# A graph layer on one core: each node's edge to itself leaves the gathered lists and is computed on the chip

## The reference

```
ht = einsum('nd,rdo->nro', h, W_rel[l])
h_rel = segment_sum(ht[src, etype], dst) + h @ W_loop[l] + b_rel[l]
z = (h @ W_gat[l]).reshape(n, H, DH)
el = sum(z * attn_l[l]);  er = sum(z * attn_r[l])
e = leaky_relu(el[src] + er[dst], 0.2)
alpha = softmax of e over the edges of one dst
h_gat = segment_sum(alpha * z[src], dst) + b_gat[l]
hc = concat([h_rel, h_gat]) @ W_fuse + b_fuse      (layer 0: hc *= sigmoid(gate))
h = relu(hc)
```

## Time and profile before

| | |
|---|---|
| runs | 3487.19 us median of 3 (3486.21 to 3488.84) |
| profiled execution, span of its instructions | 3490.2 us |
| POOL | 2489.3 us busy (71%), of them 2475 gathers with 0.95 us each |
| DVE | 2380.3 us busy (68%) |
| PE, ACT | 689.4 us (20%), 424.8 us (12%) |
| first gather of layers 0 and 1 | 214.45 us, 1315.70 us |
| mean over the 16 DMA engines | 145 GB/s |

### The profile page before, as it was taken

The page is one execution under the profiler, slowest core; times in us unless marked ns, Lnnn a source line. Parts: engine busy times, 40 slices in busy tenths (PEclk is TensorE's granted clock), DMA queues, the critical chain, the costliest instruction groups (busy, mean ns, idle before and its releaser), DMA issues.

```text
span 3490.2 us, 18122 instructions
## 1 busy us (share of the span) xinstructions
PE 689.4 (20%) x1897; PEld 372.5 (11%) x1897; DVE 2380.3 (68%) x3226; ACT 424.8 (12%) x769; POOL 2489.3 (71%) x2642
## 2 busy tenths in 40 slices
PE   8942111222122230011121111221000000000000
PEld 5421000111011110000000000110000000000000
DVE  8536666677676764665777756674776788877786
ACT  3530110111111120101111111111000000000000
POOL 1457777777777756777777777775777777777776
PEclk9965555555655555555555555555555555555555
DMA  7774444455545544444454544454433333333332
GB/s 271 315 249 129 134 147 152 152 151 152 152 152 159 168 145 118 130 151 152 151 152 151 153 152 152 152 173 140 107 106 107 107 106 107 106 106 107 106 103 74
DMA packets 143244, 505.96 MB, mean 145 GB/s; under 512 B 44277, under 2 KB 51002, under 8 KB 133618
## 3 DMA queue, kind: packets, MB, share of 16 engines
q0 software_dynamic: 130032, 444.45, 43.4%
q1 hardware_dynamic: 13186, 61.24, 4.5%
HBM read 341.05 MB, written 164.51 MB: 145 GB/s over the span
## 4 chain that ended last, share of the span: by engine, by line
POOL 45%; issue 29%; DVE 10%; DMA 6%; PE 4%; POOLq 3%; DVEq 1%; ACT 1%; SPq 1%; ACTq 0%
POOL meta_nat L594 20%; POOL late L594 14%; POOL scratch L594 10%; DVE acc L1381 3%; PE ps_table L886 1%; DMA late<-table,stage_mid 1%; DMA table<-rows 1%; DMA scratch<-table,stage_tail 1%; DVE late L1377 1%; DVE scratch L1377 1%; DVE meta_nat L1377 1%; POOLq L369 1%; POOL table L671 1%; DMA meta_nat<-table,stage_head 1%; PE ps_cnt L919 1%
## 5 line engine op out<-in xcount | busy, mean ns | idle before, releaser
L594 POOL DMA_INDIRECT meta_nat<-table,stage_head x1200 | 1139.0, 949 | 395.7 <-issue 385.3
L594 POOL DMA_INDIRECT late<-table,stage_mid x720 | 681.9, 947 | 219.4 <-issue 217.9
L594 POOL DMA_INDIRECT scratch<-table,stage_tail x555 | 525.9, 948 | 175.5 <-issue 175.2
L1025 PE MATMUL ps_mix<-ident,hr 128*128 128x128 f32 x75 | 35.5, 473 | 1991.2 <-DVE hg L1401 1991.2
L788 ACT ACTIVATE ps_cnt<-logit 128x68 f32<-128x68 f32 x189 | 43.7, 231 | 2767.1 <-DVE logit L1363 2766.1
L1381 DVE TENSOR_REDUCE acc<-meta_nat 128x132 f32<-128x2112 f32 x75 | 290.6, 3875 | 8.1 <-DVE meta_nat L1377 0.5
L1371 DVE TENSOR_REDUCE acc<-meta_nat 128x128 f32<-128x2048 f32 x75 | 282.6, 3767 | 0.0
L1049 PE MATMUL ps_table<-wrel,hT 128*128 128x512 f32 x400 | 266.4, 828 | 0.0
L1353 DVE TENSOR_TENSOR raw<-late,er_cur 128x64 f32<-128x64 f32 x45 | 12.0, 267 | 324.5 <-DMA late<-table,stage_mid 324.5
L1025 PEld LDWEIGHTS ps_mix<-ident,hr 128*128 128x128 f32 x75 | 13.6, 182 | 2039.8 <-DVE hg L1401 2039.8
L1381 DVE TENSOR_REDUCE acc<-scratch 128x132 f32<-128x1188 f32 (+1 forms) x69 | 208.7, 3024 | 7.1
(11 more groups left out here) (237 smaller groups left out, 1701.4 us busy)
## 6 DMA issues: line engine op xcount, KB each, us to landing
table<-rows SPq DMA_DIRECT2D x25, 2080.0 KB, 7.7
meta_nat<-table,stage_head POOLq DMA_INDIRECT x1200, 2.8
late<-table,stage_mid POOLq DMA_INDIRECT x720
scratch<-table,stage_tail POOLq DMA_INDIRECT x555, 2.8
meta<-meta_ranked SPq DMA_DIRECT2D x1, 2438.0 KB, 15.1
wrel<-in_L_gnn_W_rel POOLq DMA_DIRECT2D x2, 1024.0 KB, 13.5
meta_nat<-in_x SPq DMA_DIRECT2D x1, 832.0 KB, 18.4
table<-rows,stage_id POOLq DMA_INDIRECT x50, 7.8
```

The source lines that it names most:

```text
L594: pool.indirect_dma_start(out=slots[b][:, k, :], out_offset=None, in_=table[l % 2], in_offset=bass.IndirectOffsetOnAxis(ap=index, axis=0)) ...
L1025: pe.transpose(mix[0], hr[:], ident[:])
```

## The change

The last slot of a node's list is compared with the node's own rows of the table. If it is one of them, and the node's rank is 128 or more, the slot is taken out of the list and of the count, and its relation (0 to 15) is kept in a new column M_SELF of `meta`, otherwise -1. For tiles 1 to 24 of every layer:

- z and `el` of each node's own row are kept on the chip (`self_z`, in the room of `rows[1]`) and copied to slot 0 of the head buffer at the tile's start. The head group now works on 17 slots. Where a node has no dropped edge, its logit there is lowered by 1e34, which makes its weight zero.
- The own message is the row of the 16 products that M_SELF names. ScalarE copies each of the 16 products of 128x128 from PSUM with a factor of 1 or 0 for each node (`own_messages`), and TensorE sums the 16 results with identity matmuls, behind the loop product, in one bank (`own`). ScalarE copies the sum to M_LOOP of `meta` (`own_sum`), where the loop product stood.
- For layers 1 and 2 this follows `next_rows` in layers 0 and 1. For layer 0 the pass over the ranked tiles is gone; in its place `first_layer_own` makes x transposed, the products with the 16 relations, `er`, own z and own message of one tile. It runs for tiles 0 and 1 ahead of the first tile and for tile t+1 behind tile t of layer 0.
- The output `yo` lies in the room of the relation weights.

```
@@ list of the edges, on VectorE, for each of three chunks @@
+                step(v.tensor_tensor(codes, lists, is_last[:, t0:t1], ALU.mult))
+                step(v.tensor_reduce(code, codes, AX.X, ALU.add))
+                step(v.tensor_tensor(gap, code, self_at[:, t0:t1], ALU.subtract))
...
+                v.tensor_tensor(codes, is_last[:, t0:t1], bc_last(dropped[:, t0:t1], ELL), ALU.mult)
...
+                v.scalar_tensor_tensor(lists, lists, float(NULL), codes, ALU.add, ALU.subtract).then_inc(s_ell_ok, 1)
@@ ScalarE @@
-            transposed_x(1)
-            for t in range(T):
-                if t < T - 1:
-                    transposed_x(t % 2)
-                act.wait_ge(s_er_ps, t + 1)
-                s.activation(meta[:, t, M_ER:META], ps_er[t % 2], ACT.Copy).then_inc(s_er, 1)
+            def own_messages():
+                for r in range(R):
+                    m = s.activation(self_rows[:, r], ps_table[:, r * D:(r + 1) * D], ACT.Copy,
+                                     scale=type_cur[:, r:r + 1])
+                m.then_inc(s_masked, 1)
+            def own_sum(t, ready):
+                act.wait_ge(s_own_ps, n_own)
...
+                s.activation(meta[:, bass.ds(t, 1), M_LOOP:META], self_sum.rearrange("p (o f) -> p o f", o=1), ACT.Copy
+                             ).then_inc(ready, 1)
+            def first_layer_own(t):
+                s.activation(x_cur[:].rearrange("p (o f) -> p o f", o=1), meta[:, bass.ds(t, 1), M_X:M_ELL], ACT.Copy
+                             ).then_inc(s_x_cur, 1)
+                act.wait_ge(s_rank_xT, n_first)
+                s.activation(hT[1][:], xT_ranked, ACT.Copy).then_inc(s_hT[1], 1)
+                act.wait_ge(s_first_ps, n_first)
+                act.reg_add(n_first, n_first, 1)
+                own_er_and_z(t).then_inc(s_er, 1)
+                own_messages()
+                own_sum(t, s_own0)
...
+                    with act.Fori(1, T - 1) as t:
+                        tile(l, t)
+                        first_layer_own(t + 1)
@@ TensorE @@
+            def own(l, k):
+                pe.wait_ge(s_masked, n_own)
...
+                pe.matmul(self_sum, hT[k][:], wz[:, l, ER:ZW], start=True, stop=False)
+                for r in range(R):
+                    mm = pe.matmul(self_sum, ident[:], self_rows[:, r], start=False, stop=r == R - 1)
+                mm.then_inc(s_own_ps, 1)
+            def first_layer_own():
...
+                pe.transpose(xT_ranked, x_cur[:], ident[:]).then_inc(s_rank_xT, 1)
+                pe.wait_ge(s_hT[1], n_hT[1])
...
+                pe.matmul(ps_z[:, 0:ER], hT[1][:], wz[:, 0, 0:ER], start=True, stop=True)
+                for c in range(4):
+                    mm = pe.matmul(ps_table[:, 512 * c:512 * c + 512], hT[1][:],
+                                   wrel[:, 0, c * RC * D:(c + 1) * RC * D], start=True, stop=True)
+                mm.then_inc(s_first_ps, 1)
+                own(0, 1)
...
-                    z_product(l + 1, 0, ZW)
+                    z_product(l + 1, 0, ER)
...
+                    own(l + 1, 0)
@@ VectorE, start and end of a tile @@
+                v.tensor_copy(slots["H"][:, 0:1, D:ROW], self_z[:, bass.ds(t, 1), :])
...
+                if l == 0:
+                    dve.wait_ge(s_own0, n_t)
```

More of the change, by code:

```diff
@@ L21 @@
 LEAST = -1.0e37
+SHUT = -1.0e34
 SLOPE = 0.2
@@ L46, in gnn_kernel @@
     META = M_LOOP + D
-    ZW = D + H + H + D
+    EL = D + H
+    ER = EL + H
+    ZW = ER + D
     HB = 25
@@ L121, in gnn_kernel @@
         rows = [sb(f"rows{i}", [P, R, ROW]) for i in range(2)]
+        self_z = rows[1][:].rearrange("p r f -> p (r f)")[:, 0:T * EL].rearrange("p (t f) -> p t f", f=EL)
+        assert T * EL <= R * ROW
+        self_rows = sb("self_rows", [P, R, D])
+        self_room = self_rows[:].rearrange("p r d -> p (r d)")
+        is_last = self_room[:, 0:T * ELL // 2].bitcast(BF16).rearrange("p (t j) -> p t j", t=T)
+        last_at, self_at, apart, may_drop, last_code, is_self, dropped = (
+            self_room[:, T * ELL // 2 + i * T:T * ELL // 2 + (i + 1) * T] for i in range(7))
+        assert T * ELL // 2 + 7 * T <= R * D
+        self_type = sb("self_type", [P, T, R])
+        no_self = sb("no_self", [P, T])
+        type_cur = sb("type_cur", [P, R])
+        shut_cur = sb("shut_cur", [P, 1])
+        x_cur = attn_tmp
         degree = sb("degree", [P, T])
@@ L816, in next_rows @@
                     s.activation(rows[0][:, :, D:ROW], bc(ps_z[:, 0:D + H], R), ACT.Copy)
-                    for j in range(2):
-                        evacuate_half(0, j)
-                    s.activation(meta[:, bass.ds(t, 1), M_ER:META],
-                                 ps_z[:, D + H:ZW].rearrange("p (o f) -> p o f", o=1), ACT.Copy).then_inc(s_rows, 1)
+                    evacuate_half(0, 0)
+                    evacuate_half(0, 1).then_inc(s_rows, 1)
                     act.reg_add(n_tab, n_tab, 1)
+                    own_er_and_z(t)
+                    own_messages()
             n_stored = counter(act, "act_stored", 16)
@@ L855, in _ @@
                 act.wait_ge(s_saved[k], 16 * (T // 2 + 2 - k))
+            act.wait_ge(s_meta_first, 16)
+            act.wait_ge(s_own_type, 1)
+            first_layer_own(0)
+            first_layer_own(1)
+            act.wait_ge(s_meta, 16)
+            act.wait_ge(s_own_type, 2)
             n_last = counter(act, "act_last_tile", 0)
@@ L859, in _ @@
                 tile(l, 0, first=True)
-                with act.Fori(1, T) as t:
-                    tile(l, t)
+                if l == 0:
+                    with act.Fori(1, T - 1) as t:
+                        tile(l, t)
+                        first_layer_own(t + 1)
+                    tile(l, T - 1)
+                else:
+                    with act.Fori(1, T) as t:
+                        tile(l, t)
                 transposed(l)
@@ L998, in _ @@
                 natural_tile(t, t % 2, next_x=t < T - 1)
[L1001 to L1017 removed]
+            def first_layer_own():
+                pe.wait_ge(s_x_cur, n_x_cur)
+                pe.reg_add(n_x_cur, n_x_cur, 1)
+                pe.transpose(xT_ranked, x_cur[:], ident[:]).then_inc(s_rank_xT, 1)
+                pe.wait_ge(s_hT[1], n_hT[1])
+                pe.reg_add(n_hT[1], n_hT[1], 1)
+                pe.matmul(ps_z[:, 0:ER], hT[1][:], wz[:, 0, 0:ER], start=True, stop=True)
[4 more added lines that the diff above has]
+                own(0, 1)
+            n_x_cur = counter(pe, "pe_x_cur", 1)
+            pe.wait_ge(s_rows, T + 1)
+            first_layer_own()
+            first_layer_own()
             pe.wait_ge(s_bload, 16 * (5 + 3 * L))
@@ L1065, in tile @@
                 next_table(l)
-            for l in range(L):
+            with pe.Fori(2, T):
+                tile(0)
+                first_layer_own()
+            tile(0)
+            tile(0)
+            for l in range(1, L):
                 with pe.Fori(0, T):
@@ L1348, in group @@
                 lo = 1 if first else 0
+                new = 1 - lo
                 dve.wait_ge(s_landed[b], n_land[b])
```

113 lines of the change are left out of this document (73 added, 40 removed).

## The result

| | before | after |
|---|---|---|
| median of the runs | 3486.7 us (3485.4 to 3488.8) | 3606.2 us (3603.2 to 3609.8) |
| ratio | | 1.0346, 95% interval 1.0331 to 1.0360: slower by 3.5% |
| profiled span | 3490.2 us | 3608.2 us, +118.0 |
| gathers | 2475 | 2403 |
| first head gather, layer 1's, layer 2's | 214.45, 1315.70, 2411.8 | 219.49, 1478.21, 2557.04 |

The account below looks back on a forecast made before the run. It took GpSimd's gathers as the bound (2475 x 1.25 = 3097 us). Layer 0 and start +203.1, layer 1 -30.0 and +10.3, layer 2 -30.0 and +0.3 gave +154: 3641 us, range 3504 to 3800.

Parts of the forecast that it names:

- The ring: Layer 0, one head exponential to the next through ScalarE and TensorE: 56.1 us for three-group tiles, 46.0 for two.
- The 15.3: Layer 0's two-group tiles, from the head's exponential to the end of the row copies, table product included: 15.3 us.
- The sum of 17: TensorE's 17 matmuls of 128x128 that sum the masked copies: 7.4 us, bounds 5.2 and 10.3.
- The masked copy: ScalarE's 128x128 copies with a factor per node: 0.25 us each, 4.1 us for 16.
- Layer 0's product: TensorE's product of tile t+1 with all relations, at the high clock: 4.3 us, bounds 4.0 and 7.6.
- the 30.7: Layer 0, own work after the row copies until the next head's exponential: 12.4 plus 18.3, together 30.7 us.
- The start: Before the gathers, 6.7 us of VectorE list work under 7.0 us of cover; second head's gathers at 262.2, not 251.61.
- Layers 1 and 2: Each layer gains 30.0 us from fewer gathers; layer 1's end adds 10.3, layer 2's last group 0.3.
- the clock's rival: TensorE's clock stays at 1.2 GHz in every burst: 3859 us, chance 0.10.
- The first rival: TensorE keeps its high clock, masked copies overlap, the chain hides behind the gathers: 3418 us, chance 0.10.
- the slots don't fall: Rival that lists get no shorter: +60 us in layers 1 and 2, 3701 us, chance 0.03.
- each us counts 48 times: Each us on a sum or on the 16 copies counts 48 times in the kernel's time, on the product 24 times.

Follow-up runs that it names:

- hidden2: Changed kernel with layer 0 reordered, the ranked tile's masked rows and sum in their own buffer and PSUM region, same results: 3433.2 us, 0.9842 of the kernel before.
- after_again: The changed kernel measured once more, nothing altered: 3607.7 us, 1.0338 of the kernel before.
- no_first_b: Changed kernel without the 16 masked copies and 16 identity matmuls of the first layer's own step: 3470.7 us, 0.9947 of the kernel before.
- no_msgs_b: Changed kernel without masked copies and identity matmuls in all layers: 3917.4 us (no_msgs 3912.3), on chips where the kernel before takes 3969.
- no_drop: Changed kernel with all own work but no list shortened: 4843.9 us, 1.2201 of the kernel before there; the same kernel on the faster chip 3675.8 us, 1.0536.

## Why the prediction was right, by its own steps

The direction, the mechanism and the place held; the size was 36 us of span too large (+154 forecast, +118.0 measured).

- **The ring** was forecast as "head exponential, 15.3, row copies, 30.7, head exponential". Measured 14.14 and 30.24, so 44.4 us for 46.0, and 54.6 for 56.1. Ten and twelve turns make 35 of the 40.6 us by which layer 1 starts earlier than forecast (+162.5, not +203.1); 2.8 came before the first turn, 2.7 at the layer's end.
- **The 15.3** was too long by the table's product. I took 6.75 us from its first instruction to the last row copy's start, from the end of layer 0. It has 5.6 (TensorE's L947 at 1217.07, the copy at 1222.70). The row chosen was the longest of its kind: the product takes 6.18 us there at a granted clock of 0.58, but 4.75 at 0.76 within the layer, and the 25 of layer 0 before lie between 4.51 and 6.18, with a mean of 5.36. In the changed kernel they lie between 4.72 and 5.13. The prediction had both rows and took the dearer one.
- **The sum of 17**: 7.4 forecast, 6.7 and 6.6 us measured from its first instruction to the copy's start at 1235.52 and 1252.73. That it came out so near is partly luck, since two terms were off in opposite ways. The burst from 1228.80 stays at a granted clock of 0.50 until 1234.0, 5.2 us and not the 4.4 assumed; its instructions are cheaper than assumed, 20 in the first 4.2 us at that clock, 0.42 us a matmul for 0.59. In hidden2, where the clock was at 1.00 throughout the sum, 34 instructions took 3.8 us, 0.11 each and so 0.22 a matmul for my 0.29; that is a quarter of the 0.45 that an instruction of 512 columns has at 1.00 in the changed kernel (L1092, eight in 3.60 us). The rule of the Trainium skill (TensorE: Matmul & The Clock Gate, Step-by-step: what each phase is for) that weight loads are pulled ahead gave an estimate of 6.3 us in the prediction (from the terms given there it is 6.1); the measurement lies between it and 7.4, and in the stream of hidden2 the trace agrees with the rule.
- **The masked copy**: 4.24 us for 16, forecast 4.1; a single one takes 0.42, the next follows 0.255 later. The estimate of 0.29 by the Trainium skill (ScalarE: Activation LUTs, What ACT_TABLE_LOAD costs) is 14% more than the trace has, so keeping the row's 0.25 was right.
- **Layer 0's product**: 4.45 us from the copy of hT to the next copy, forecast 0.3 + 4.3, at a granted clock of 1.00 as assumed.
- **Forgotten**: from the start of the last copy to the exponential it is 1.13 us, 0.85 of it idle; I had 0.2 for both. The two sums, 0.7 and 0.8 shorter, hide that, so that the 30.7 came out within 0.5.
- **The start**: 7.0 us of cover for 6.7 of list work was "just enough". It was not in the profiled execution: `stage_head` is ready at 218.43, 11.0 us later than before, and the first gather waits for it and comes 5.0 us later. How much of this the list work costs isn't fixed by one execution: after_again, the same kernel, has `stage_head` at 210.28 and its first gather at 217.42, and in the other kernels of its set the first gather comes between 214.37 and 217.56. The second head's gathers at 261.26 (262.2 forecast) hide most of it: the own work of tiles 0 and 1 was later still.
- **Layers 1 and 2**: -17.3 and -27.2 for -19.7 and -29.7. With as many gathers, the end of layer 1 is 8.6 us longer (10.3 forecast) and that of layer 2 is 3.9 shorter (0.3 longer forecast). Against this, the turns take 4.4 and 6.8 us more beyond their gathers, most of it in the last tiles: the last two turns take 34.2 to 34.4 us with one gather less, and 33.9 to 34.0 before, so dropping the slot brings nothing there.
- **Chances**: the clock's rival (always 1.2 GHz) fails on the windows: the product of the ranked tile runs at 1.00, and a sum starts at 0.50 and ends at the high clock. The first rival (3418) fails in both its conditions: the sums run at a mean clock of 0.60 and the masked copies follow each other after 0.255 us. Its number was also wrong by its own terms, since 206 us less than 3641 are 3435 and the gathers can only cut off a part of that gain. That hidden2 comes to 3433 is by another mechanism, a changed order, and doesn't bear it out. That the slots don't fall is excluded by 2403 gathers.

What the prediction did not see is VectorE's parallel path, which limits what a shorter sum can gain: its "each us counts 48 times" holds only as far as that path. 10 us less a turn in layer 0 would be 240 us by it, and no_first_b, the run without them, gave 137.

## What to carry to other kernels

Work that is put on idle engines costs nothing only if it doesn't close a ring: follow a full turn through every engine's program order, with each handover, and compare it with the turn of the bound engine. If the turn is longer, look first for the buffer or the sum that makes one engine wait for the other, not for faster instructions: a second buffer and a later copy gave 174 us here, with as many instructions. Removing part of a chain brings no more than the distance to the next path beside it.

## What the hardware showed that was not expected

- TensorE's sums of 128x128 in float32 ran at 0.11 us an instruction in layer 0 of hidden2, where they follow other matmuls without a pause (45 of them, each 3.74 us for its 32 instructions), and at 0.18 to 0.19 behind a pause of 5 to 6 us in the changed kernel. Windows of two such bursts, hidden2 and the changed kernel (us, busy us of PE, PEld, DVE, ACT, POOL, granted clock):
```profile
1055.10:1059.10 4.00, 4.00 (x36) 3.83 (x34) 3.14 (x8) 2.16 (x3) 3.05 (x4) 1.00 0.42 120
```
```profile
1229.36:1235.37 6.01, 6.00 (x33) 5.81 (x32) 2.68 (x7) 0.00 (x0) 4.49 (x6) 0.60 0.36 102
```
  The first came right behind 5.3 us of products, the second behind 6.1 us of idle time and the sum's first matmul, at 0.60 of full speed on average: 0.50, which is 1.2 GHz, until 1234.0, and 0.96 in the last 1.4 us. The place in the program sets the price.
- On two of the three chips of the sets the kernel before took 14% longer. No trace of it was taken there; in the traces of its variants there the instructions take as long as elsewhere (gathers of 947 ns) and the loss stands in every layer, in layer 2 too, where no own message is made: its first two turns have 36.3 and 55.0 us in no_msgs_b as in the changed kernel on the faster chip, but the third and fourth 65.9 and 68.3 in place of 51.3 and 48.7. In no_drop the waits stand in front of instructions whose releaser was done or that the trace does not name. In layer 2 they begin with the turn of the third tile, in layer 1 with the same or (no_msgs, no_msgs_b) the one after; the third tile is the second pass through the loops of ScalarE and VectorE. That the jump back has to do with them was not tried, and their cause stays open. The own work cost 5.4% on one chip and 22% on the other; that a tight ring is what makes it suffer more is likely and not shown.
